# The first product's input: rounded to 16-bit integers on ScalarE, widened on GpSimd, transposed by a DMA, in straight code

## What is computed

```python
x = x + xattn(layernorm(x), ctx)          # the mask leaves each query one row or an even mean
h = layernorm(layernorm(x)) * gamma + beta
xq = clip(round(h * 127 / max|h|), -128, 127)       # per token
wq = clip(round(w1 / mean|w1|), -1, 1)              # per matrix
h = gelu(xq @ wq.T / scales + b1)                   # 512 -> 2048
hq = clip(round(h * 127 / max|h|), -128, 127)       # per token
out = x + hq @ w2q.T / scales + b2                  # 2048 -> 512
```

## Time and profile before

| | us |
|---|---|
| median of 3 runs | 596.81 (595.59 to 597.13) |
| span of the profiled execution | 593.9 |
| TensorE busy | 567.0 (95%) |
| VectorE busy | 516.0 (87%) |
| GpSimd busy | 449.4 (76%) |
| ScalarE busy | 434.7 (73%) |

### The profile page before, as it was taken

The page is one execution under the profiler, slowest core; times in us unless marked ns, Lnnn a source line. Parts: engine busy times, 40 slices in busy tenths (PEclk is TensorE's granted clock), DMA queues, the critical chain, the costliest instruction groups (busy, mean ns, idle before and its releaser), DMA issues.

```text
span 593.9 us, 10522 instructions
## 1 busy us (share of the span) xinstructions
PE 567.0 (95%) x3374; PEld 294.6 (50%) x3438; DVE 516.0 (87%) x803; ACT 434.7 (73%) x412; POOL 449.4 (76%) x584
## 2 busy tenths in 40 slices
PE   7979787999999999999999999999999999999996
PEld 3434333555555555555555555555555555555553
DVE  0286999999999999999999999999999999998773
ACT  0047854888787778878877878777887887787784
POOL 0007789999888888888988888988888898887410
PEclk9989888999999999999999999999999999999999
DMA  9987311222221122222112222212212211200001
GB/s 320 410 317 264 115 38 53 72 72 73 71 72 48 61 71 71 71 71 70 45 62 71 71 71 71 59 50 68 71 71 71 71 53 54 87 36 19 37 35 54
DMA packets 26408, 52.87 MB, mean 89 GB/s; under 512 B 2728, under 2 KB 2728, under 8 KB 25748
## 3 DMA queue, kind: packets, MB, share of 16 engines
q1 hardware_dynamic: 24708, 49.25, 25.0%
q10 hardware_dynamic: 1680, 3.36, 1.5%
HBM read 35.60 MB, written 17.00 MB: 89 GB/s over the span
## 4 chain that ended last, share of the span: by engine, by line
PE 84%; DVE 7%; DMA 3%; issue 2%; POOL 1%; ACT 1%; ACTq 1%; POOLq 0%
PE p_y L773 36%; PE p_ffn L758 34%; PE p_hT L745 9%; DMA xb<-ctxT 3%; PE p_xT L695 2%; DVE hid L579 1%; DVE hmax L586 1%; PE p_y L715 1%; DVE wpart L516 1%; POOL x L297 1%; ACTq L407 1%; DVE hx L535 1%; DVE stat L551 1%; DVE w2q L511 1%; DVE xb L484 0%
## 5 line engine op out<-in xcount | busy, mean ns | idle before, releaser
L773 PE MATMUL p_y<-w2q,hqT 128*128 128x512 bf16 x1023 | 234.8, 383 | 7.0 <-DVE y L661 3.5
L758 PE MATMUL p_ffn<-w1q,xqT 128*128 128x512 bf16 x961 | 219.6, 381 | 6.9 <-ACT xqT L423 3.7
L466 ACT ACTIVATE hround<-hid,hscale 128x2048 f32<-128x2048 f32 x64 | 128.2, 2003 | 76.0 <-DVE hscale L592 76.0
L579 DVE SCALAR_TENSOR_TENSOR hid<-p_ffn,xdeq,b_b 128x1024 f32<-128x1024 f32 x128 | 163.5, 1280 | 2.8 <-issue 0.7
L773 PEld LDWEIGHTS p_y<-w2q,hqT 128*128 128x128 bf16 x1024 | 98.2, 99 | 116.1 <-issue 5.5
L758 PEld LDWEIGHTS p_ffn<-w1q,xqT 128*128 128x128 bf16 x1024 | 97.8, 98 | 111.3 <-ACT xqT L423 3.7
L445 ACT ACTIVATE hid<-hid 128x1024 f32<-128x1024 f32 x128 | 134.6, 1052 | 19.7 <-DVE hid L579 19.7
L586 DVE TENSOR_REDUCE hmax<-hid 128x1 f32<-128x2048 f32 x64 | 145.7, 2276 | 0.1
L459 ACT ACTIVATE hqT<-p_hT 128x1024 bf16<-128x1024 int16 x128 | 123.9, 1020 | 17.2 <-PE p_hT L745 16.6
L297 POOL TENSOR_TENSOR x<-x,attn 128x512 f32<-128x512 f32 x64 | 81.5, 1275 | 44.7 <-ACT attn L429 44.7
L311 POOL TENSOR_TENSOR hx<-hx,beta_b 128x512 f32<-128x512 f32 x63 | 80.5, 1278 | 4.9
(11 more groups left out here) (58 smaller groups left out, 284.0 us busy)
## 6 DMA issues: line engine op xcount, KB each, us to landing
x<-x SPq DMA_DIRECT2D x64, 256.0 KB, 2.8
out<-y SPq DMA_DIRECT2D x64, 256.0 KB, 2.9
raw<-w2T SPq DMA_DIRECT2D x4, 1024.0 KB, 8.9
raw<-wout ACTq DMA_DIRECT2D x8, 256.0 KB, 7.0
raw<-wvT SPq DMA_DIRECT2D x8, 256.0 KB, 6.5
hid<-w1T SPq DMA_DIRECT2D x2, 1024.0 KB, 15.4
hround<-w1T SPq DMA_DIRECT2D x2, 1024.0 KB, 20.4
attn<-tail_rows SPq DMA_DIRECT2D x7, 256.0 KB
```

What stands on the lines that cost most here:

```text
L466: nc.scalar.activation(hround[:, (c - 1) % 2, :], hid[:, (c - 1) % 2, :], ACT.Copy, scale=col(hscale, c - 1), bias=MAGIC).then_inc(hround_ ...
L579: nc.vector.scalar_tensor_tensor(hid[:, c % 2, h * HALF:(h + 1) * HALF], p_ffn1[:, h * HALF:(h + 1) * HALF], col(xdeq, c), b1_b[:, h * HAL ...
L758: mm = nc.tensor.matmul(p_ffn1[:, n * D:(n + 1) * D], xqT[:, c % 2, k, :], w1q[:, k, n * D:(n + 1) * D], start=(k == 0), stop=(k == KD - 1))
L773: mm = nc.tensor.matmul(p_y[:, :], hqT[:, c % 2, k, :], w2q[:, k, :], start=(k == 0), stop=(k == KH - 1))
```

## The change

The 16-bit rounding no longer uses `MAGIC` for the first product. ScalarE multiplies `hx` by the scale and writes int16 into a new tile `xint` (`round_x`, the conversion rounds). GpSimd copies it to bf16 into `xq`, two slots (`narrow_x`, in the place of `round_h`; it first waits for `xscale` and makes `xdeq`, then waits for the rounding). SyncE starts a transposing DMA from `xq` into `xqT`, and TensorE waits for its landing; `transpose_h` and `evac_x` are gone.

ScalarE's new operation stands behind the second gelu of the step, for tile s+2. In SyncE's step the transpose of tile s+1 comes first (it waits for the first product of s-1 and for `xq`), then the store, then the load, which stood ahead of the store. The transposes of tiles 0 and 1 stand behind the transfers that spread the attention rows. VectorE's waits for the transposes become waits for the rounding. `ones`, the matrix of ones for the weights' sum, moves into an unused corner of `y`, and TensorE waits for `ident` in the first step with a transpose. `run` is straight code for all steps, on all engines.

```diff
@@ run
-            for c in range(first, BODY):
-                step(0, c)
-            with eng.Fori(1, TURNS - 1) as i:
-                for c in range(BODY):
-                    step(i, c)
-            for c in range(BODY):
-                step(TURNS - 1, c)
-            for c in range(3):
-                step(TURNS, c)
+            for s in range(first, T + 3):
+                step(s // BODY, s % BODY)
@@ SyncE
             for b in range(1, B):
                 spread_tail(b)
 
+            def transpose_x(t, c):
+                sp.wait_ge(xq_ready, t + 1)
+                sp.dma_start_transpose(xqT[:, c % 2, :, :], xq[:, c % 2, :]).then_inc(xqT_loaded[c % 2], 16)
+
+            for t in range(2):
+                transpose_x(t, t)
+
             def step(i, c):
                 s = BODY * i + c
-                if live(i, c, 8):
-                    sp.wait_ge(xb_ready, s + 1)
-                    sp.dma_start(x1[:, c, :], x[bass.ds((s + 8) * P, P), :]).then_inc(x_loaded[c], 16)
+                if live(i, c, 1) and live(i, c, -1):
+                    sp.wait_ge(ffn1_done, 2 * s)
+                    transpose_x(s + 1, c + 1)
                 if live(i, c, -3):
                     sp.wait_ge(y_ready, s - 2)
                     sp.dma_start(out[bass.ds((s - 3) * P, P), :], y[:, (c - 3) % 4, :])\
                         .then_inc(y_stored[(c - 3) % 4], 16)
+                if live(i, c, 8):
+                    sp.wait_ge(xb_ready, s + 1)
+                    sp.dma_start(x1[:, c, :], x[bass.ds((s + 8) * P, P), :]).then_inc(x_loaded[c], 16)
@@ GpSimd
-            def round_h(t, c):
+            def narrow_x(i, c):
+                t = BODY * i + c
                 pool.wait_ge(xscale_ready, t + 1)
                 pool.tensor_tensor(col(xdeq, c), col(xstep, c), wmean[:, 0:1], ALU.mult)\
                     .then_inc(xdeq_ready, 1)
-                h = hx[:, c % 4, :]
-                pool.tensor_scalar(h, h, col(xscale, c), MAGIC, ALU.mult, ALU.add)\
-                    .then_inc(xround_done, 1)
+                pool.wait_ge(xround_done, t + 1)
+                if live(i, c, -2):
+                    pool.wait_ge(xqT_loaded[c % 2], halves(i, c - 2))
+                pool.tensor_copy(xq[:, c % 2, :], xint[:, :]).then_inc(xq_ready, 1)
@@ ScalarE
-            def evac_x(t, c):
-                act.wait_ge(xT_done, t + 1)
-                nc.scalar.activation(xqT[:, c % 2, :, :], p_xT[:, :, 0:P].bitcast(I16),
-                                     ACT.Copy, bias=-float(OFFSET)).then_inc(xqT_ready, 1)
+            def round_x(i, c):
+                t = BODY * i + c
+                act.wait_ge(xscale_ready, t + 1)
+                if live(i, c, -1):
+                    act.wait_ge(xq_ready, t)
+                nc.scalar.activation(xint[:, :], hx[:, c % 4, :], ACT.Copy,
+                                     scale=col(xscale, c)).then_inc(xround_done, 1)
@@ ScalarE, start and step
-            evac_x(0, 0)
+            round_x(0, 0)
             round_weights(1, 0)
+            round_x(0, 1)
             round_weights(1, 1)
...
                 if live(i, c, 0):
                     gelu(s, c, 0)
-                if live(i, c, 1):
-                    if live(i, c, -1):
-                        act.wait_ge(ffn1_done, 2 * s)
-                    evac_x(s + 1, c + 1)
                 if live(i, c, 0):
                     gelu(s, c, 1)
+                if live(i, c, 2):
+                    round_x(i, c + 2)
@@ VectorE, step
                     if live(i, c, -1):
-                        dve.wait_ge(xT_done, s)
+                        dve.wait_ge(xround_done, s)
                     standardise(s + 3, c + 3)
@@ TensorE, step
-                    pe.wait_ge(xqT_ready, s + 1)
+                    pe.wait_ge(xqT_loaded[c % 2], halves(i, c))
...
-                if live(i, c, 1):
-                    pe.wait_ge(xqT_ready, s + 1)
-                    transpose_h(s + 1, c + 1)
```

More of the change, by code:

```diff
@@ L94, in block_program @@
         hx = sb("hx", [P, 4, D])
+        xint = sb("xint", [P, D], I16)
+        xq = sb("xq", [P, 2, D], BF16)
         xqT = sb("xqT", [P, 2, KD, P], BF16)
@@ L132, in block_program @@
         wscale = sb("wscale", [P, 2])
-        ones = sb("ones", [P, P])
+        ones = y[:, 1, P:2 * P]
         p_ffn1 = ps("p_ffn1", [P, HID])
@@ L173, in block_program @@
         xdeq_ready, xround_done = sem("xdeq_ready"), sem("xround_done")
-        xT_done, xqT_ready = sem("xT_done"), sem("xqT_ready")
+        xq_ready = sem("xq_ready")
+        xqT_loaded = [sem(f"xqT_loaded{r}") for r in range(2)]
         ffn1_done, bias_done, gelu_done = sem("ffn1_done"), sem("bias_done"), sem("gelu_done")
@@ L184, in col, with halves @@
             return t[:, c % 8:c % 8 + 1]
+        def halves(i, c):
+            return 16 * (4 * i + c // 2 + 1)
         def live(i, c, ahead):
@@ L276, in _ @@
         def _(pool):
-            pool.memset(ones[:, :], 1.0).then_inc(ones_set, 1)
+            pool.memset(ones, 1.0).then_inc(ones_set, 1)
             pool.memset(neg_half[:, :], -0.5).then_inc(ones_set, 1)
@@ L349, in _ @@
             pool.wait_ge(wmean_done[0], 1)
-            round_h(0, 0)
+            narrow_x(0, 0)
             first_sum(2)
             first_sum(3)
-            round_h(1, 1)
+            narrow_x(0, 1)
             first_factor(2)
@@ L357, in _ @@
             affine(2, 2)
-            round_h(2, 2)
+            narrow_x(0, 2)
             affine(3, 3)
             first_sum(5)
-            round_h(3, 3)
+            narrow_x(0, 3)
             first_factor(4)
@@ L373, in _ @@
                 pool.wait_ge(attn_spread[b], 64 if b else 48)
-            round_h(4, 4)
+            narrow_x(0, 4)
             first_sum(7)
@@ L382, in step @@
                 if live(i, c, 1) and live(i, c, -4):
-                    round_h(s + 1, c + 1)
+                    narrow_x(i, c + 1)
                 n, r = i + (c + 6) // BODY, (c + 6) % BODY
@@ L447, in _ @@
             gelu(0, 0, 0)
-            evac_x(1, 1)
             gelu(0, 0, 1)
+            round_x(0, 2)
             round_weights(1, 3)
@@ L633, in _ @@
             clip(1, 2)
-            dve.wait_ge(xT_done, 1)
+            dve.wait_ge(xround_done, 1)
             first_standardise(4)
@@ L642, in _ @@
             first_scale(4)
-            dve.wait_ge(xT_done, 2)
+            dve.wait_ge(xround_done, 2)
             first_standardise(5)
@@ L690, in _ @@
         def _(pe):
[L691 to L696, removed]
             for k in range(KI):
@@ L708, in _ @@
             pe.wait_ge(wsum_done[0], 1)
-            nc.tensor.matmul(p_wsum[:, 0:1], ones[:, :], wsum[:, 0:1], start=True, stop=True)\
+            nc.tensor.matmul(p_wsum[:, 0:1], ones, wsum[:, 0:1], start=True, stop=True)\
                 .then_inc(wtotal_done[0], 1)
@@ L727, in _ @@
                     if b == B - 1 and k == 1:
-                        pe.wait_ge(ident_set, 2)
-                        transpose_h(0, 0)
                         pe.wait_ge(wsum_done[1], 1)
-                        nc.tensor.matmul(p_wsum[:, D:D + 1], ones[:, :], wsum[:, 1:2], start=True, stop=True)\
+                        nc.tensor.matmul(p_wsum[:, D:D + 1], ones, wsum[:, 1:2], start=True, stop=True)\
                             .then_inc(wtotal_done[1], 1)
@@ L740, in step @@
                         pe.wait_ge(wmean_done[1], 1)
+                        pe.wait_ge(ident_set, 2)
                     else:
```

## The result

| | before | after |
|---|---|---|
| median of the runs, us | 596.21 (595.59 to 597.13) | 600.75 (600.12 to 602.12) |
| span of the profiled execution, us | 593.9 | 598.3 |
| first `bias` of VectorE, us | 62.59 | 73.85 |
| first load of the first even step, us | 98.10 | 113.45 |
| last of the even steps, us | 571.48 | 575.92 |

The changed kernel is slower by 0.6%: the ratio on record is 1.0059, 95% interval 1.0039 to 1.0079. It is not the quotient of the two medians of the table, which is 1.0076; the four runs of the kernel before in it are on the short side, and by the median of its 17 later runs (597.46 us) the quotient is 1.0055. The forecast was 595.6 us, slightly faster than before, with chances of 0.35 for faster, 0.22 for the same and 0.43 for slower. So the sum had the wrong sign, while "slower" had the largest chance. The range, 587.5 to 608, holds the time.

What follows compares the result with a forecast made beforehand. TensorE was taken to set the pace at 8.02 us a step, with VectorE close behind. The profiled 593.9 + 10.0 at the start - 11.2 in the steps + 2.9 to the median gave 595.6 us, range 591.2 to 600.9.

Steps and rivals of the forecast that it cites:

- at no cost: SyncE's queue: store and load behind the waiting transpose are late by less than a step, costing nothing.
- the half clock: TensorE's first product after idling: 1.7 us to the first bias, up to 3.4 at half speed; 2.6 taken.
- The gain per step: Even steps: period falls from 8.02 to 7.83 us, 11.2 us gained over 59 steps, bounds 9.4 to 13.0.
- S: Start of VectorE's standardisation (L535), 306.23 us in the trace before; GpSimd's narrowing was to start at S + 1.66.
- the same law: VectorE's standardisation blocked behind GpSimd's L311: 2P = 15.02 + c, P the period, c the narrowing's length (0.70 us taken).
- The removed transposes: TensorE: four transposing matmuls and their loads a step, worth 0.22 us; 13.0 us over 59 steps if TensorE stays the bound.
- The loops: Straight code in place of loops: nothing on TensorE, up to 0.1 us a step on VectorE.
- the runs' time: Median of the runs taken as 2.9 us over the profiled span, added to 592.7 us.
- The queue at the start: SyncE's first two transposes queue behind the attention-row transfers; tile 0 lands near 70.0 us, first bias 10.0 us late (7.4 to 13.5).
- the start costs little: Rival at the start: transposes don't queue behind the spread rows, bias only some 2 us late, 587.6 us; chance 13%.
- The transpose's time: Transposing DMA takes 2.0 us, upper end 4.5, hidden under 6.8 us; four in a row by the skill page 5.2 us.
- slow in every step: Rival in the even steps: the transposing DMA decides from 6.8 us; at 9 us, time about 669 us; chance 10%.

Runs made afterwards that it cites:

- the first experiment: Changed kernel with SyncE's transposes of tiles 2 to 4 issued ahead of the loads of tiles 8 to 11: 596.23 us, ratio 0.9983 to the kernel before.

## Why the prediction missed the sign

**What failed: SyncE's order in the first steps, put at nothing.** The words were that the store and the load behind the transpose are late by less than a step, "at no cost". The prediction asked what is queued behind the waiting transpose in SyncE's queue. It did not ask what the transpose is queued behind. In an even step the load ahead of it (of the step before) is released in time. In the first steps it is not: the load of step 0 waits for `xb` of tile 0, which GpSimd finishes only at 88.87 + 1.71 = 90.58 us, while tile 2 is ready to be transposed at 79.48. The first `xb` in the timelines, kernel before and kernel after:

```profile
76.89 1.71 POOL L329 TENSOR_TENSOR xb<-x,b_b 128x512 f32<-128x512 f32 x1
```

```profile
88.87 1.71 POOL L341 TENSOR_TENSOR xb<-x,b_b 128x512 f32<-128x512 f32 x1
```

Before the change the load waited in the same way, until 78.60 us, but nothing that TensorE needed soon stood behind it. The term was put at 0; the traces give 4.09 us, and with the loads moved 3.4 us of it are back (the span is 3.9 shorter, the time 0.76% less). With this term the forecast's sum would have been 595.6 + 4.1 = 599.7 us, against 600.75 measured. With the wait taken out of the kernel instead, the first experiment, the ratio is 0.9983, where the forecast had 595.6 / 596.81 = 0.998. The measured time is inside the forecast's own bounds (591.2 to 600.9 us) only by 0.15 us, and that is luck: they have no term for this hole.

**What was mis-sized: the half clock.** The first product started at 70.10 us, forecast 70.0. From there to `bias` I took 2.6 us, the middle of 1.7 and 3.4; it took 3.75. TensorE had stood still for 11 us, and the granted clock is 0.50 in every stretch up to 74 us. The rows of before showed 0.63 and 0.52 after a shorter idle stretch, so the upper end, 3.4, was the value to take; even that is short, since the loads followed each other at 0.43 us. This is 1.15 of the 1.26 us that the start came later than forecast in this execution; the scatter of the start is larger than that.

**What was right.** The gain per step: 10.91 us against 11.2 (the step 7.84 against 7.83). Its terms were each a little off and cancelled: the narrowing took 0.61 us and not 0.70, the rounding on ScalarE 0.71 and not 0.58, so the narrowing began at S + 1.70 and not S + 1.66. With 0.61 and 1.70 the same law gives 7.84. What the prediction did not see is that the steps alternate, 7.60 and 8.07; their mean is the law's. The rows show that the law leaves this open. From the start of a standardisation to the end of the next turn's L321 it is 303.54 - 295.12 = 8.42 us, and from an end of L321 to the next standardisation 303.27 - 296.02 = 7.25. So two turns together are 15.67 us, twice 7.84, however they are divided, as long as both end on L321. What picks the division was not tested. The removed transposes are worth 0.22 us a step, as taken from the last steps of before: with GpSimd out of the way the step is 7.80. The loops: nothing. The end: nothing. One smaller reading was off: the runs' time lies 1.8 us over the span of the same execution, not 2.9; the other 1.1 us are that the profiled execution of before was shorter than the median run.

**The queue at the start.** Right in mechanism and size: with the transposes behind the spread rows the first product starts at 70.10 us, ahead of them at 61.28, and by the medians the move is worth 600.75 - 591.28 = 9.5 us against 10.0 forecast. The rival "the start costs little" is thereby excluded for this kernel, and shown for the one with the order changed, where that rival's 587.6 us and the third transpose's 4.1 make 591.7, and 591.28 was measured. That it fits so closely is partly luck, with the scatter of the start.

**The transpose's time.** 2.4 us from issue to landing at the median of 64, inside the 2.0 to 4.5 taken and under the 6.8 that cover it; the rival in which it is slow in every step is excluded. The list of waits has no wait of TensorE for `xqT` in the even steps. The estimate of 5.2 us, worked out from the Trainium skill (VectorE: DVE Perf Modes, "The three transpose paths"), is contradicted, at least if four pieces are taken as four in a row. The distribution of the kernel after, issue to landing:

```profile
DMA to landing us min/median/max: 2.4/2.4/10.8
```

Its longest, 10.8 us, is among the two that stood in line with the spread rows (7.6 and 10.8). In that line the forecast's "under 7 us" does not hold.

## What to carry to other kernels

When an instruction with a deadline is put into an in-order queue, look at both sides of it: who waits behind it, and which wait stands ahead of it, in the first steps as well as in an even one, for a queue that was late at no cost becomes costly when something urgent joins it. When one engine's instruction moves by a microsecond, look where all that follows it on that engine now lands: here VectorE's standardisation, started while GpSimd's L321 ran, ended only 0.28 us after it, and filling GpSimd's wait with other work brought back all of the 0.04 us a step. Not all work of the two is coupled so: VectorE's `bias` at 293.78 us, kernel after, ran beside two such GpSimd operations in 1.27 us, and took 1.28 at 73.85 us with GpSimd idle. A gain per step and a loss at the start are settled by different edits; here two changes in the order of a queue turned a loss of 0.6% into a gain of 1.6%.

## What the hardware showed that I had not expected

- A transposing DMA of 128x512 values of 16 bits, SBUF to SBUF, keeps SyncE's queue for 1.20 us to issue, where a plain 256 KB load or store takes 0.33 to 0.58, and lands in 2.4 us. It costs many packets: the execution has 61,251 in place of 26,408, with 37,544 of them under 512 bytes. With other transfers under way the first two take 6.56 us to issue. TensorE did the same work in 0.22 us a step of its own time.
- VectorE and GpSimd, meeting at one operation in every turn, settled into an alternation, 8.07 and 7.60 us, whose mean the simple sum gave; with the narrowing doubled VectorE got past GpSimd for fourteen steps before they collided.
- GpSimd's int16 to bf16 copy of 128x512 takes 0.61 us, little less than the f32 multiply and add on one input, 0.70. ScalarE's f32 to int16 rounding of the same size takes 0.71 us, more than the int16 read-out of PSUM that it replaced, 0.58; the two differ in their source, their types and the scale read from a tile, and which of these costs the 0.13 was not tested.
